# Order of the last overlapped turn and of the tail in a fused two-layer gated cross-attention kernel: one output projection, one turning step and half an output product in other places

## The chip, the cores and the metric

The kernel runs on one core of one Trainium2 chip. The metric is the time of one execution in microseconds (us), from device timestamps; lower is better. Besides that time there is one execution taken by the hardware profiler. Its span runs from the first to the last instruction, and its own time is a little longer than its span.

## The reference

The input is x, of shape 8 x 256 x 512 (eight batches), and a context of the same shape. Four residual layers follow each other, each with a layer norm before it and tanh of a gate as its factor:

```python
x = x + tanh(g_xattn[0]) * L0_xattn(layernorm(x), ctx, ctx)   # causal attention, 16 heads of 32
x = x + tanh(g_ffn[0])   * L0_ffn(layernorm(x), ...)          # ternary weights, 512 -> 2 x 2048 -> 512
x = x + tanh(g_xattn[1]) * L1_xattn(layernorm(x), ctx, ...)   # q projection, rms norms, softmax, output projection
x = x + tanh(g_ffn[1])   * L1_ffn(layernorm(x), ...)          # 8-bit activations, ternary weights
```

The last layer is what the tail of the kernel computes: the normed input is scaled by 127 over its largest absolute value and rounded, multiplied with ternary weights into a value and a gate of 2048 columns each, u = value * silu(gate); u is scaled and rounded in the same way (which needs the largest absolute value over a whole row) and multiplied with ternary output weights.

## The kernel before, in words

There are four stages, a to d, one for each layer. Stages c (second attention) and d (last feed-forward) are interleaved: in a turn, attention of batch b, the output projection of batch c = b-1 and the feed-forward of batch d = b-2 run side by side. Turns 3 to 7 are a loop; the eighth turn is written out, with b = 7, c = 6, d = 5, and no further batch to prepare. Behind it comes the tail, in which batches 6 and 7 pass through the feed-forward. A batch has 256 rows, that is two tiles of 128 (t = 0, 1).

Each engine has its own program, in which every instruction stands in the order written by hand and waits on semaphores. TensorE's program names these steps; each has a counterpart with its name, or a related one, on VectorE (DVE) and ScalarE (ACT):

- c_scores(b, g): attention scores of four heads, group g of 4, into banks 0 to 3; VectorE takes row maxima (L1652).
- c_max_turn(b): the negated maxima, turned (L763). VectorE's c_max_parts prepares them and c_max_rows (L1667) copies the turned ones back.
- c_probs(b, g): scores again, transposed (L773) plus maxima (L777), for four heads; ScalarE takes the exponentials in two instructions (L1192).
- c_weigh(b, g): weighted values and sums (L792); VectorE divides (L1683 reciprocal, L1685 product).
- c_project_out(b, t): output projection (L699), 4 matmuls of 128x512 f32, recorded as 8. VectorE adds it to x (c_add_out, L1690).
- d_value_gate(d, j), j = 0 to 7: 4 matmuls for a gate and 4 for a value (L804), 512 columns, four j for each tile. ScalarE makes silu of the gate (d_gate, L1209), VectorE the product u (L1753) and after every second j a maximum over 1024 columns (L1759).
- d_scale_u (L1765 to L1769): the scale of u from those maxima, six dependent small instructions. ScalarE's d_round_u (L1221) scales and rounds, in two halves of 1024 columns; VectorE's d_integers16 (L1778) writes them as 16-bit.
- d_turn_u(d, t): 16 transposes (L434) of the rounded u, eight to a bank (steps ut t.0 and ut t.1); ScalarE copies each bank out (d_turn_u, L1227, recorded under the helper's line L1012).
- d_out_product(d, t, first, end): 16 matmuls (L834) of the output product, or one half of them; the second eight need the second copy. VectorE's d_store (L1797) adds to x, and SyncE stores it.

PSUM has 8 banks. Banks 0 to 3 belong to the scores and probabilities until the eighth turn ends. The strings in places.turn give the order in which the steps take banks 4 to 7 (one string for each bank; w0 is c_weigh 0's, mt c_max_turn's, po c_project_out's, ut d_turn_u's). A step waits until the step named before it in the same string has been read out. The list ends does the same for the tail, going round all eight banks. The step before in the string is therefore a wait, wherever it is read late:

```python
def d_turn_u(d, t, n):                                        # ScalarE, L1223
    act.wait_ge(s.d_ut, 4 * d + 2 * t + n + 1)
    copy(UT[d, t][:, n * 1024:(n + 1) * 1024], ...).then_inc(s.d_utr, 1)
```

In the eighth turn ScalarE's program is: exponentials 0, a rounding, exponentials 1, a rounding, exponentials 2, a rounding, exponentials 3, then the copies of d_turn_u.

Of the kernel before, what the change touches and what calls it, by code (L numbers as in the profile page):

```python
# [17 lines left out]
KH = HID // P  # L18
NB = 8
# [6 lines left out]
NG = NH // 4  # L26
# [126 lines left out]
def build(nc, x, ctx, ctxT, gates, w0, w1, wkv, wqo, vec, wnorm, cols, cst, masks, selq, selc, out):  # L153
    with ExitStack() as stack:
# [112 lines left out]
        for turn in range(3, NB):  # L267
            places.turn(turn, ("g0 v1 g3 pq0 v6 v7 ut0.0 y0 xt0", "v0 po1 v3 g4 v5 g7 tq1 w1 w2 w3", "po0 g2 kt0 v4 pq1 w0 qt1 ut1.1 y1",
                               "g1 v2 kt1 g5 g6 mt tq0 ut0.1 qt0 ut1.0 xt1"))
        places.turn(NB, ("g0 v1 g3 v5 v7 w1 w3", "v0 po1 v3 g6 g7 ut0.0 y0", "po0 g2 g4 g5 mt w0 ut0.1", "g1 v2 v4 v6 w2"))  # L270
        places.last.update({n: (s.c_ex, 8 * NB) for n in range(4)})
        a, b, c = NB - 3, NB - 2, NB - 1
        ends = ([("po0", c), ("ut1.0", a), ("ut1.1", a), ("po1", c), ("qt0", b), ("qt1", b), ("y1", a)]
                + [(f"{what}{j}", b) for j in range(6) for what in "gv"] + [("qt0", c), ("qt1", c)]
                + [(f"{what}{j}", b) for j in (6, 7) for what in "gv"] + [("g0", c), ("v0", c), ("g1", c), ("v1", c)]
                + [("ut0.0", b), ("ut0.1", b), ("g2", c), ("v2", c), ("y0", b), ("g3", c), ("v3", c), ("ut1.0", b), ("ut1.1", b), ("g4", c), ("v4", c)]
                + [("g5", c), ("v5", c), ("ut0.0", c), ("ut0.1", c), ("g6", c), ("v6", c), ("g7", c), ("v7", c)]
                + [("y1", b), ("y0", c), ("ut1.0", c), ("ut1.1", c), ("y1", c)])
        for k, (name, batch) in enumerate(ends):
            places.put((0, 1, 2, 3, 4, 6, 7, 5)[k % 8], name, batch)  # L280

# [149 lines left out]
        def tensor_program(pe):  # L431
# [278 lines left out]
            def c_project_out(b, t):  # L710
                pe.wait_ge(s.c_pvr, 4 * b + 4)
                c_product(f"po{t}", b, bufC["OT"], t, "o").then_inc(s.c_po, 1)
# [31 lines left out]
            def c_scores(b, g):  # L744
                QT, KT = (bufW[n][:, b % 2 * KD + g, :] for n in ("QT", "KT"))
                pe.wait_ge(s.c_qtr, 4 * b + 4)
                pe.wait_ge(s.c_ktr, 2 * b + 2)
                pe.wait_ge(s.c_scr, 4 * b + g)
                if b == 0:
                    pe.wait_ge(s.b_h, 8 * NB)  # L750
                pe.wait_ge(s.c_ex, 8 * b)
                for t in range(TB):
                    for j in range(4):
                        mm = pe.matmul(banks[j][:, t * S:(t + 1) * S], part(QT, j)[:, t * P:(t + 1) * P], part(KT, j),  # L754
                                       start=(t == 0), stop=(t == 1), skip_group_check=True)
                mm.then_inc(s.c_sc, 1)

            def c_max_turn(b):
                to, sem, value = bank_c("mt", b)
                pe.wait_ge(sem, value)  # L760
                pe.wait_ge(s.c_mhl, b + 1)
                for t in range(TB):
                    mm = pe.transpose(as16(to, BF16)[:, t * P:(t + 1) * P], bufC["MHL"][:, t, :], keep["identb"])  # L763
                mm.then_inc(s.c_mt, 1)
# [31 lines left out]
            def d_value_gate(d, j):  # L796
                t, n = j // 4, j % 4
                pe.wait_ge(s.d_qtr, 2 * d + t + 1)
                for name, col, done in ((f"g{j}", HID + n * D, s.d_g), (f"v{j}", n * D, s.d_gu)):
                    to, sem, value = bank_c(name, d)  # L800
                    pe.wait_ge(sem, value)
                    for k in range(KD):
                        at = k * 2 * HID + col
                        mm = pe.matmul(to, QQ[d][:, t, k * P:(k + 1) * P], W1[:, at:at + D],  # L804
                                       start=(k == 0), stop=(k == KD - 1))
                    mm.then_inc(done, 1)
# [155 lines left out]
            c_project_out(c, 0)  # L962
            d_value_gate(d, 1)
            c_scores(b, 1)
            c_project_out(c, 1)
            d_value_gate(d, 2)
            c_scores(b, 2)
            d_value_gate(d, 3)
            d_value_gate(d, 4)
            c_scores(b, 3)  # L970
            d_value_gate(d, 5)
            d_value_gate(d, 6)
            c_max_turn(b)
            d_value_gate(d, 7)
            for g in range(NG):
                c_probs(b, g)
                if g:
                    c_weigh(b, g - 1)
            d_turn_u(d, 0)
            c_weigh(b, 3)  # L980
            d_out_product(d, 0)
            c_project_out(b, 0)
            d_turn_u(d, 1)
            c_project_out(b, 1)
# [13 lines left out]
            d_turn_u(c, 1)  # L998
            d_value_gate(b, 4)
            d_value_gate(b, 5)  # L1000
            d_turn_u(b, 0)
            d_value_gate(b, 6)
            d_value_gate(b, 7)
            d_out_product(c, 1)
            d_out_product(b, 0, 0, KH // 2)
            d_turn_u(b, 1)
            d_out_product(b, 0, KH // 2)
            d_out_product(b, 1)

        def scalar_program(act):  # L1010
# [309 lines left out]
            d_gate(d, 1)  # L1320
            d_residual(d, 0)
            d_residual(d, 1)
            for j in range(2, 8):
                d_gate(d, j)
            warm(ACT.Exp)
            c_probs(b, 0)
            d_round_u(d, 0, 0)
            c_probs(b, 1)
            d_round_u(d, 0, 1)
            c_probs(b, 2)  # L1330
            d_round_u(d, 1, 0)
            c_probs(b, 3)
            warm(ACT.Silu)
            both(d_turn_u, d, 0)
            d_round_u(d, 1, 1)
            both(d_turn_u, d, 1)
            d_residual(c, 0)
            d_residual(c, 1)
# [25 lines left out]
        def vector_program(v):  # L1364
# [381 lines left out]
                    v.tensor_scalar(bufC["q16"][:, t, :], bufC["h"][:, t, :], MAGIC, 127.0, ALU.subtract, ALU.min).then_inc(s.d_q, 1)  # L1746

            def d_value_gate(d, j):
                t, n = j // 4, j % 4
                v.wait_ge(s.d_sv, d + 1)  # L1750
                v.wait_ge(s.d_gu, 8 * d + j + 1)
                v.wait_ge(s.d_sg, 8 * d + j + 1)
                v.scalar_tensor_tensor(out=bufW["u"][:, t, n * D:(n + 1) * D], in0=bank_c(f"v{j}", d)[0], scalar=keep["sv"][:, d % 2, t:t + 1],  # L1753
                                       in1=bufC["SG"][:, n % 2, :], op0=ALU.mult, op1=ALU.mult).then_inc(s.d_u, 1)
                apart = (d, t) == (NB - 1, 1) and n > 1
                if n % 2 or apart:
                    first, m = (n, n - 1) if apart else (n - 1, n // 2)
                    v.wait_ge(s.d_u, 8 * d + j + 1)
                    v.tensor_reduce(keep["um"][:, t, m:m + 1], bufW["u"][:, t, first * D:(n + 1) * D], AX_X, ALU.max, apply_absolute_value=True).then_inc(*own.up())  # L1759
# [205 lines left out]
            c_add_out(c, 0)  # L1965
            d_value_gate(d, 1)
            c_scores(b, 1)
            c_add_out(c, 1)
            v.wait_ge(s.c_xo, 2 * c + 2)
            d_spread(c)  # L1970
            d_value_gate(d, 2)
            c_scores(b, 2)
            d_value_gate(d, 3)
            d_value_gate(d, 4)
            c_scores(b, 3)
            c_max_parts(b)
            d_scale_u(d, 0)
            d_value_gate(d, 5)
            c_max_rows(b)
            d_value_gate(d, 6)  # L1980
            d_value_gate(d, 7)
            d_scale_u(d, 1)
            d_weighted(c)
            c_weigh(b, 0)
            d_integers16(d, 0)
            c_weigh(b, 1)
            d_peak(c)
            c_weigh(b, 2)
            c_weigh(b, 3)
            d_inputs(c)  # L1990
            d_integers16(d, 1)
            d_store(d, 0)
            c_add_out(b, 0)
            c_add_out(b, 1)
# [208 lines left out]
```

## Time and profile before

| what | us |
|---|---|
| median of three runs | 1124.33 |
| lowest and highest | 1123.89, 1126.89 |
| the profiled execution's own time | 1122.95 |
| its span | 1121.0 |
| TensorE (PE) busy | 1093.6 |
| VectorE (DVE) busy | 832.5 |
| ScalarE (ACT) busy | 567.4 |

A row of the timeline has start, length (both us), engine, line, operation, output<-inputs and shape, and a count where like instructions are merged; in brackets the idle time of the engine before it and what ended it. Merged matmuls overlap: the start of the next row, not the length, tells when the engine went on. A row of the windows gives busy time of an engine and number of instructions begun, and PEclk, the granted TensorE clock (1.00 is 2.4 GHz, 0.50 is 1.2 GHz).

### The profile page before, as it was taken

How to read it: one execution, taken by the hardware profiler on the slowest of the kernel's cores; microseconds unless marked ns; L12 is line 12 of the kernel's file. 1: busy time of each engine (PE TensorE's matmuls, PEld its weight loads, DVE VectorE, ACT ScalarE, POOL GpSimd, SP SyncE). 2: the span in 40 equal slices, each digit the busy share in tenths (PEclk: the TensorE clock that was granted, in tenths of full speed). 3: DMA queues.
4: the chain of work that ended last, by engine and by line, in shares of the span. 5: the costliest groups of instructions: out<-in, count | busy, mean ns of one | idle time of the engine just before them, and what ended most of it. 6: DMA issues, size and time to landing. Idle time of an engine off the chain costs nothing.

```text
span 1121.0 us, 25577 instructions
## 1 busy us (share of the span) xinstructions
PE 1093.6 (98%) x10386; PEld 661.7 (59%) x10386; DVE 832.5 (74%) x1437; ACT 567.4 (51%) x918; POOL 117.3 (10%) x212
## 2 busy tenths in 40 slices
PE   8899999999999999999999999999999999999998
PEld 3455555556777777777777655555554545454543
DVE  4888888778676657566565667986868787778795
ACT  4767666765433323333333352464554547372654
POOL 1101100110000000000001122120202020201010
PEclk9999999999999999999999999999999999999999
DMA  9655555433212011021010201101010101000001
GB/s 361 205 188 182 187 190 174 147 107 124 67 39 66 20 39 38 20 76 38 20 58 20 85 1 39 39 2 57 1 58 1 58 1 39 1 11 10 11 10 38
DMA packets 29267, 79.24 MB, mean 71 GB/s; under 512 B 3040, under 2 KB 3296, under 8 KB 28896
## 3 DMA queue, kind: packets, MB, share of 16 engines
q1 hardware_dynamic: 29152, 77.61, 21.2%
q8 instruction: 84, 1.38, 0.5%
q14 instruction: 31, 0.25, 0.1%
HBM read 65.02 MB, written 12.58 MB: 69 GB/s over the span
## 4 chain that ended last, share of the span: by engine, by line
PE 91%; DVE 4%; ACT 2%; issue 2%; DMA 1%; SPq 0%; POOL 0%; ACTq 0%; DVEq 0%; POOLq 0%
PE bank L699 10%; PE bank L593 10%; PE bank L594 10%; PE bank L681 10%; PE bank L554 9%; PE bank L804 9%; PE bank L434 5%; PE bank L834 5%; PE bank L792 5%; PE bank L754 3%; PE bank L773 3%; PE bank L486 2%; PE bank L459 2%; PE bank L507 2%; PE bank L519 2%
## 5 line engine op out<-in xcount | busy, mean ns | idle before, releaser
L593 PE MATMUL bank<-ARENA,W 128*128 128x256 f16 x1024 | 227.3, 273 | 0.7 <-issue 0.7
L594 PE MATMUL bank<-ARENA,W 128*128 128x256 f16 x1024 | 227.3, 273 | 0.0
L1012 ACT ACTIVATE ARENA<-bank 128x512 f32<-128x512 f32 (+3 forms) x143 | 93.0, 687 | 71.7 <-PE bank L434 31.8
L681 PE MATMUL bank<-W,ARENA 128*128 128x512 bf16 x512 | 120.8, 379 | 0.0
L804 PE MATMUL bank<-W,ARENA 128*128 128x512 bf16 x512 | 119.3, 383 | 0.4 <-DVE W L1753 0.4
L554 PE MATMUL bank<-ARENA 128*128 128x512 f32 x256 | 117.8, 602 | 0.7 <-DMA ARENA<-in_wkv 0.7
L699 PE MATMUL bank<-ARENA 128*128 128x512 f32 x256 | 116.9, 599 | 0.0
L593 PEld LDWEIGHTS bank<-ARENA,W 128*128 128x128 bf16 x1024 | 100.2, 98 | 19.1 <-issue 1.3
L594 PEld LDWEIGHTS bank<-ARENA,W 128*128 128x128 bf16 x1024 | 100.2, 98 | 18.0
L1012 ACT ACTIVATE ARENA<-ARENA 128x512 f16<-128x512 f32 x64 | 40.3, 630 | 133.2 <-DVE ARENA L1607 129.5
L2031 POOL TENSOR_TENSOR ARENA<-ARENA 128x2 f32<-128x2 f32 (+1 forms) x72 | 49.6, 689 | 507.1 <-DVE ARENA L1387 267.4
L1607 DVE SCALAR_TENSOR_TENSOR ARENA<-bank,ARENA 128x512 f32<-128x512 f32 x64 | 48.0, 750 | 72.5 <-PE bank L594 69.1
L1209 ACT ACTIVATE ARENA<-bank,ARENA 128x512 f32<-128x512 f32 x64 | 43.7, 685 | 109.1 <-PE bank L804 101.3
L804 PEld LDWEIGHTS bank<-W,ARENA 128*128 128x128 bf16 x512 | 49.2, 99 | 67.1 <-issue 15.0
L1130 ACT ACTIVATE ARENA<-bank 128x512 f32<-128x512 f32 x64 | 38.2, 597 | 91.1 <-PE bank L594 91.1
L1652 DVE TENSOR_REDUCE ARENA<-bank 128x4 f32<-128x1024 f32 x64 | 75.2, 1218 | 9.4 <-PE bank L754 9.4
L1613 DVE TENSOR_TENSOR ARENA<-ARENA 128x512 f16<-128x512 f32 x64 | 44.2, 691 | 47.3 <-ACT ARENA L1012 47.3
L554 PEld LDWEIGHTS bank<-ARENA 128*128 128x128 f32 x256 | 46.6, 190 | 54.7 <-issue 51.1
L681 PEld LDWEIGHTS bank<-W,ARENA 128*128 128x128 f16 x512 | 50.0, 99 | 48.7 <-issue 1.9
L1683 DVE RECIPROCAL ARENA<-bank 128x256 f32<-128x256 f32 x32 | 56.2, 1755 | 29.5 <-PE bank L792 29.2
L1397 DVE TENSOR_REDUCE ARENA<-bank 128x4 f32<-128x512 f32 x64 | 58.2, 951 | 26.5 <-PE bank L459 26.5
L699 PEld LDWEIGHTS bank<-ARENA 128*128 128x128 f32 x256 | 46.6, 190 | 52.6 <-issue 51.6
(181 smaller groups left out, 1801.9 us busy)
## 6 DMA issues: line engine op xcount, KB each, us to landing
W<-in_w SPq DMA_DIRECT2D x48, 512.0 KB, 4.3
ARENA<-in_w SPq DMA_DIRECT2D x24, 512.0 KB, 3.6
kv_store<-ARENA SPq DMA_DIRECT2D x32, 256.0 KB, 4.3
W<-kv_store SPq DMA_DIRECT2D x15, 512.0 KB, 4.0
ARENA<-in_ctxT SPq DMA_DIRECT2D x8, 512.0 KB, 3.8
X<-in_x SPq DMA_DIRECT2D x8, 512.0 KB, 6.1
ARENA<-in_ctx SPq DMA_DIRECT2D x8, 512.0 KB, 6.1
out<-X SPq DMA_DIRECT2D x16, 256.0 KB, 2.0
```

The costliest lines, as they stand in the source:

```text
L434: mm = pe.transpose(to[:, k * P:(k + 1) * P], tile, one)
L554: mm = pe.matmul(bank, bufA["KT"][:, b % 2 * KD + k, t * P:(t + 1) * P], W[:, k, :], start=(k == 0), stop=(k == KD - 1))
L593: pe.matmul(bank[:, i * S:(i + 1) * S], W0[:, at:at + P], xt_half(b, 0)[:, k, :], start=(k == 0), stop=False)
L594: mm = pe.matmul(bank[:, i * S:(i + 1) * S], W0[:, at:at + P], xt_half(b, 1)[:, k, :], start=False, stop=(k == KD - 1))
L681: mm = pe.matmul(banks[6 + t], hx(q, what)[:, i * S + t * P:i * S + (t + 1) * P], W0[:, UP_AT + m * D:UP_AT + (m + 1) * D], start=(m == 0 ...
L699: mm = pe.matmul(to, src[:, k, t * P:(t + 1) * P], WQ[w][:, k, :], start=(k == 0), stop=(w == "o" and k == KD - 1))
L792: mm = pe.matmul(part(to, j)[:, what * S:(what + 1) * S], lhs, bufC["PT"][:, h % 8, kb * S:(kb + 1) * S], start=(kb == 0), stop=True, skip ...
L804: mm = pe.matmul(to, QQ[d][:, t, k * P:(k + 1) * P], W1[:, at:at + D], start=(k == 0), stop=(k == KD - 1))
L1012: return act.activation(to, src, ACT.Copy)
L1397: got = v.tensor_reduce(NM[:, t, :, g % 2], bank[:, 0:4, t * P:t * P + (t + 1) * P], AX_X, ALU.max, negate=True)
L1652: got = v.tensor_reduce(NM[:, t, :, g], bank[:, 0:4, t * S:(t + 1) * S], AX_X, ALU.max, negate=True)
L1683: v.reciprocal(bufC["rec"], to[:, S:2 * S]).then_inc(*own.up())
```

## The change

In the eighth turn, c_project_out(6, 1) moves from behind scores 1 to behind c_max_turn. d_turn_u(5, 0) moves from behind weighing 2 to between probabilities 0 and probabilities 1, and the first half of the output product of (5, 0) to before weighing 3. On ScalarE the two roundings of (5, 0) move from between the exponentials to before gates 6 and 7, the two copies of the turned values to between exponentials 1 and 2, and the roundings of (5, 1) behind the exponentials. VectorE's order follows; d_value_gate is split there into the product and the maximum. The bank strings of the turn change with it: po1 goes behind g7 in bank 5, and in bank 6 ut0.1 now stands before w0. In the tail, the first half of the output product of (6, 1) moves before d_turn_u(7, 0), and the output product of (7, 0) stands whole before d_turn_u(7, 1), of which its second half was the successor. In the list ends, ("y1", b) moves forward, which shifts the banks of all that come after it: ut1.0 of batch 7 now follows y1 of batch 6 in bank 2.

```diff
--- before.py
+++ after.py
@@ -267,15 +267,15 @@
         for turn in range(3, NB):
             places.turn(turn, ("g0 v1 g3 pq0 v6 v7 ut0.0 y0 xt0", "v0 po1 v3 g4 v5 g7 tq1 w1 w2 w3", "po0 g2 kt0 v4 pq1 w0 qt1 ut1.1 y1",
                                "g1 v2 kt1 g5 g6 mt tq0 ut0.1 qt0 ut1.0 xt1"))
-        places.turn(NB, ("g0 v1 g3 v5 v7 w1 w3", "v0 po1 v3 g6 g7 ut0.0 y0", "po0 g2 g4 g5 mt w0 ut0.1", "g1 v2 v4 v6 w2"))
+        places.turn(NB, ("g0 v1 g3 v5 v7 w1 w3", "v0 v3 g6 g7 po1 ut0.0 y0", "po0 g2 g4 g5 mt ut0.1 w0", "g1 v2 v4 v6 w2"))
         places.last.update({n: (s.c_ex, 8 * NB) for n in range(4)})
         a, b, c = NB - 3, NB - 2, NB - 1
         ends = ([("po0", c), ("ut1.0", a), ("ut1.1", a), ("po1", c), ("qt0", b), ("qt1", b), ("y1", a)]
                 + [(f"{what}{j}", b) for j in range(6) for what in "gv"] + [("qt0", c), ("qt1", c)]
                 + [(f"{what}{j}", b) for j in (6, 7) for what in "gv"] + [("g0", c), ("v0", c), ("g1", c), ("v1", c)]
                 + [("ut0.0", b), ("ut0.1", b), ("g2", c), ("v2", c), ("y0", b), ("g3", c), ("v3", c), ("ut1.0", b), ("ut1.1", b), ("g4", c), ("v4", c)]
-                + [("g5", c), ("v5", c), ("ut0.0", c), ("ut0.1", c), ("g6", c), ("v6", c), ("g7", c), ("v7", c)]
-                + [("y1", b), ("y0", c), ("ut1.0", c), ("ut1.1", c), ("y1", c)])
+                + [("g5", c), ("v5", c), ("y1", b), ("ut0.0", c), ("ut0.1", c), ("g6", c), ("v6", c), ("g7", c), ("v7", c)]
+                + [("y0", c), ("ut1.0", c), ("ut1.1", c), ("y1", c)])
         for k, (name, batch) in enumerate(ends):
             places.put((0, 1, 2, 3, 4, 6, 7, 5)[k % 8], name, batch)
 
@@ -962,23 +962,24 @@
             c_project_out(c, 0)
             d_value_gate(d, 1)
             c_scores(b, 1)
+            d_value_gate(d, 2)
+            d_value_gate(d, 3)
+            c_scores(b, 2)
+            d_value_gate(d, 4)
+            d_value_gate(d, 5)
+            c_scores(b, 3)
+            d_value_gate(d, 6)
+            d_value_gate(d, 7)
+            c_max_turn(b)
             c_project_out(c, 1)
-            d_value_gate(d, 2)
-            c_scores(b, 2)
-            d_value_gate(d, 3)
-            d_value_gate(d, 4)
-            c_scores(b, 3)
-            d_value_gate(d, 5)
-            d_value_gate(d, 6)
-            c_max_turn(b)
-            d_value_gate(d, 7)
-            for g in range(NG):
+            c_probs(b, 0)
+            d_turn_u(d, 0)
+            for g in range(1, NG):
                 c_probs(b, g)
-                if g:
-                    c_weigh(b, g - 1)
-            d_turn_u(d, 0)
+                c_weigh(b, g - 1)
+            d_out_product(d, 0, 0, KH // 2)
             c_weigh(b, 3)
-            d_out_product(d, 0)
+            d_out_product(d, 0, KH // 2)
             c_project_out(b, 0)
             d_turn_u(d, 1)
             c_project_out(b, 1)
@@ -998,13 +999,13 @@
             d_turn_u(c, 1)
             d_value_gate(b, 4)
             d_value_gate(b, 5)
+            d_out_product(c, 1, 0, KH // 2)
             d_turn_u(b, 0)
             d_value_gate(b, 6)
             d_value_gate(b, 7)
-            d_out_product(c, 1)
-            d_out_product(b, 0, 0, KH // 2)
+            d_out_product(c, 1, KH // 2)
+            d_out_product(b, 0)
             d_turn_u(b, 1)
-            d_out_product(b, 0, KH // 2)
             d_out_product(b, 1)
 
         def scalar_program(act):
@@ -1320,19 +1321,19 @@
             d_gate(d, 1)
             d_residual(d, 0)
             d_residual(d, 1)
-            for j in range(2, 8):
+            for j in range(2, 6):
                 d_gate(d, j)
+            both(d_round_u, d, 0)
+            d_gate(d, 6)
+            d_gate(d, 7)
             warm(ACT.Exp)
             c_probs(b, 0)
-            d_round_u(d, 0, 0)
             c_probs(b, 1)
-            d_round_u(d, 0, 1)
+            both(d_turn_u, d, 0)
             c_probs(b, 2)
-            d_round_u(d, 1, 0)
             c_probs(b, 3)
             warm(ACT.Silu)
-            both(d_turn_u, d, 0)
-            d_round_u(d, 1, 1)
+            both(d_round_u, d, 1)
             both(d_turn_u, d, 1)
             d_residual(c, 0)
             d_residual(c, 1)
@@ -1746,12 +1747,19 @@
                     v.tensor_scalar(bufC["q16"][:, t, :], bufC["h"][:, t, :], MAGIC, 127.0, ALU.subtract, ALU.min).then_inc(s.d_q, 1)
 
             def d_value_gate(d, j):
+                d_gated(d, j)
+                d_largest(d, j)
+
+            def d_gated(d, j):
                 t, n = j // 4, j % 4
                 v.wait_ge(s.d_sv, d + 1)
                 v.wait_ge(s.d_gu, 8 * d + j + 1)
                 v.wait_ge(s.d_sg, 8 * d + j + 1)
                 v.scalar_tensor_tensor(out=bufW["u"][:, t, n * D:(n + 1) * D], in0=bank_c(f"v{j}", d)[0], scalar=keep["sv"][:, d % 2, t:t + 1],
                                        in1=bufC["SG"][:, n % 2, :], op0=ALU.mult, op1=ALU.mult).then_inc(s.d_u, 1)
+
+            def d_largest(d, j):
+                t, n = j // 4, j % 4
                 apart = (d, t) == (NB - 1, 1) and n > 1
                 if n % 2 or apart:
                     first, m = (n, n - 1) if apart else (n - 1, n // 2)
@@ -1965,30 +1973,31 @@
             c_add_out(c, 0)
             d_value_gate(d, 1)
             c_scores(b, 1)
+            d_value_gate(d, 2)
+            d_value_gate(d, 3)
+            c_scores(b, 2)
+            d_scale_u(d, 0)
+            d_value_gate(d, 4)
+            d_gated(d, 5)
+            c_scores(b, 3)
+            c_max_parts(b)
+            d_largest(d, 5)
+            d_gated(d, 6)
+            c_max_rows(b)
+            d_integers16(d, 0)
+            d_value_gate(d, 7)
             c_add_out(c, 1)
+            d_scale_u(d, 1)
             v.wait_ge(s.c_xo, 2 * c + 2)
             d_spread(c)
-            d_value_gate(d, 2)
-            c_scores(b, 2)
-            d_value_gate(d, 3)
-            d_value_gate(d, 4)
-            c_scores(b, 3)
-            c_max_parts(b)
-            d_scale_u(d, 0)
-            d_value_gate(d, 5)
-            c_max_rows(b)
-            d_value_gate(d, 6)
-            d_value_gate(d, 7)
-            d_scale_u(d, 1)
+            c_weigh(b, 0)
             d_weighted(c)
-            c_weigh(b, 0)
-            d_integers16(d, 0)
             c_weigh(b, 1)
             d_peak(c)
             c_weigh(b, 2)
             c_weigh(b, 3)
+            d_integers16(d, 1)
             d_inputs(c)
-            d_integers16(d, 1)
             d_store(d, 0)
             c_add_out(b, 0)
             c_add_out(b, 1)
```

## Rows read from the trace of the kernel before

**Rows 1.** The page, section 1: busy time and its share of the span.
```profile
PE 1093.6 (98%) x10386; PEld 661.7 (59%) x10386; DVE 832.5 (74%) x1437; ACT 567.4 (51%) x918; POOL 117.3 (10%) x212
```

**Rows 2.** Waits of TensorE, 900 to 1121 us: us in total, times, longest.
```profile
PE bank L434 <- DVE ARENA L1778: 2.0, 2, 1.6
PE bank L773 <- ACT ARENA L1192: 1.8, 3, 1.3
PE bank L792 <- DVE ARENA L1685: 1.3, 1, 1.3
PE bank L773 <- DVE ARENA L1667: 0.4, 1, 0.4
PE bank L804 <- DVE W L1753: 0.4, 1, 0.4
```

**Rows 3.** Timeline of TensorE in the eighth turn.
```profile
1036.60 1.15 PE L773 MATMUL bank<-W 32*128 32x256 f32 x16 [0.41 <-DVE ARENA L1667]
...
1039.24 1.74 PE L773 MATMUL bank<-W 32*128 32x256 f32 x14 [1.28 <-ACT ARENA L1192]
...
1041.35 1.07 PE L792 MATMUL bank<-ARENA,W 128*32 128x256 f32 x16
...
1049.96 1.07 PE L434 MATMUL bank<-ARENA 128*128 128x128 bf16 x16
1050.96 1.07 PE L792 MATMUL bank<-ARENA,W 128*32 128x256 f32 x16
1051.85 1.05 PE L792 MATMUL bank<-ARENA 128*32 128x256 f32 x16
1052.83 3.63 PE L834 MATMUL bank<-W,ARENA 128*128 128x512 bf16 x16
1056.29 3.60 PE L699 MATMUL bank<-ARENA 128*128 128x512 f32 x8
```

**Rows 4.** Timeline of ScalarE in the eighth turn: exponentials 1, a rounding, two copies.
```profile
1041.45 1.94 ACT L1192 ACTIVATE ARENA<-bank 128x1024 f32<-128x1024 f32 x2 [0.40 <-PE bank L777]
1043.27 1.15 ACT L1221 ACTIVATE W<-W,ARENA 128x1024 f32<-128x1024 f32 x1
...
1051.56 1.92 ACT L1012 ACTIVATE ARENA<-bank 128x1024 bf16<-128x1024 bf16 x2
```

**Rows 5.** Timeline of VectorE: division after weighing 3; one scan of scores.
```profile
1030.50 2.35 DVE L1652 TENSOR_REDUCE ARENA<-bank 128x4 f32<-128x1024 f32 x2
...
1052.96 1.76 DVE L1683 RECIPROCAL ARENA<-bank 128x256 f32<-128x256 f32 x1 [0.65 <-PE bank L792]
1054.75 0.42 DVE L1685 TENSOR_TENSOR ARENA<-bank,ARENA 128x256 f32<-128x256 f32 x1
```

**Rows 6.** Timeline of TensorE in the tail.
```profile
1094.41 3.62 PE L804 MATMUL bank<-W,ARENA 128*128 128x512 bf16 x16
1099.64 0.61 PE L434 MATMUL bank<-ARENA 128*128 128x128 bf16 x8 [1.61 <-DVE ARENA L1778]
1100.68 0.61 PE L434 MATMUL bank<-ARENA 128*128 128x128 bf16 x8 [0.43 <-DVE ARENA L1778]
1101.12 5.30 PE L804 MATMUL bank<-W,ARENA 128*128 128x512 bf16 x16
1106.26 5.34 PE L834 MATMUL bank<-W,ARENA 128*128 128x512 bf16 x24
1111.44 1.06 PE L434 MATMUL bank<-ARENA 128*128 128x128 bf16 x16
1112.34 5.34 PE L834 MATMUL bank<-W,ARENA 128*128 128x512 bf16 x24
```

**Rows 7.** Timeline of VectorE and ScalarE in the tail.
```profile
1106.52 0.75 DVE L1753 SCALAR_TENSOR_TENSOR W<-bank,ARENA 128x512 f32<-128x512 f32 x1 [0.50 <-PE bank L804]
...
1111.30 0.74 DVE L1797 SCALAR_TENSOR_TENSOR X<-bank,ARENA,X 128x512 f32<-128x512 f32 x1
...
1112.09 1.02 ACT L1012 ACTIVATE ARENA<-bank 128x1024 bf16<-128x1024 bf16 x1 [1.64 <-PE bank L434]
```

**Rows 8.** Windows of TensorE: us, busy, granted clock (PEclk), DMA share, GB/s.
```profile
1003.00:1006.00 3.00, 1.66 (x33) 1.00 0.03 5
1038.00:1041.00 3.00, 1.63 (x20) 1.00 0.00 0
1101.50:1104.50 3.00, 3.00 (x9) 0.50 0.00 0
1104.85:1106.26 1.41, 1.41 (x8) 1.00 0.00 0
```

**Rows 9.** The only earlier fall of the clock: a timeline row, then two windows.
```profile
35.71 0.30 PE L444 MATMUL bank<-ARENA 32*128 32x64 bf16 x16 [2.35 <-ACT ARENA L1012]
...
34.00:36.00 2.00, 0.29 (x20) 1.00 0.61 94
36.00:38.00 2.00, 1.90 (x30) 0.61 0.92 348
```

## What the change should do to the time

> **What bounds the kernel now.** I read the page's busy times first. TensorE is busy for 1093.6 of 1121.0 us, 98% [rows 1], so a reordering can gain only what TensorE stands still or runs slowly around the edit. The waits of TensorE from 900 us on give the stock [rows 2]. In the eighth turn these are 0.39 us before value 7, 0.41 us for the turned maxima and 1.28 us for the exponentials; in the tail 1.61 and 0.43 us for the rounded values. The 1.3 us behind a division lies at 1004 us, ahead of the edit, and stays. The timeline then shows the places [rows 3, 6]. The windows show something no wait row does: from about 1101.5 to 1104.8 us the granted clock is 0.50, the 1.2 GHz level [rows 8]. Sixteen matmuls that start at 1101.12 go on to 1106.26, that is 5.14 us [rows 6]; at full clock 24 take 1106.26 to 1111.44 = 5.18 us, 0.216 each, so 16 take 3.45. The slow stretch costs 1.69 us. What came before it was 1.61 and 0.43 us of idleness within 2.65 us.
>
> **The eighth turn up to probabilities 0: about nothing.** The output projection (3.43 to 3.5 us, the row of its sister at 1056.29 is followed by transposes 3.43 us later) moves behind the maxima, where it covers VectorE's copy of them (the 0.41 us wait). In exchange everything between comes 3.45 us earlier and meets VectorE and ScalarE. VectorE scans each of the four scores for 2.35 us [rows 5], and ScalarE now does two roundings of 1.04 us each (a rounding of 1.15 us, pipelined) before gate 6. Played through in order from the second scan, which starts at 1019.96 in both: scan 2.27, two products and a maximum 2.6, scan 2.27, scale 1.2 brings the scale to 1028.3, two roundings to 1030.4, silu of gate 6 to 1031.1. TensorE would have got to gate 7 at 1030.1 and needs the bank of gate 6: 1.0 us idle. From 1031.2: value and gate 7 1.73, maxima 0.25, projection 3.45 gives 1036.65 for probabilities 0, against 1036.60 now [rows 3]. The two short waits are only replaced by one of 1.0 us. Bounds: minus 0.8 us (no new wait), plus 0.7 us; I take 0.05.
>
> **Turned values between the probabilities: a new wait of 3.9 us.** This decides. Bank 6 is now read by ut0.1 before w0 takes it. Weighing 0 thus waits for ScalarE's second copy, and in ScalarE's program both copies stand behind exponentials 1. Exponentials 1 need probabilities 1, whose matmuls need exponentials 0, so they start when they do now, at 1041.45, and the next instruction of ScalarE starts at 1043.27 [rows 4]. The two copies take 1.92 us [rows 4]: 1045.19, and 0.06 until TensorE goes on, 1045.25. TensorE's own work up to weighing 0 ends at 1041.35, where weighing 0 starts now [rows 3]; the transposes (1.0 us) fit into the stretch in which it waits for the exponentials anyway, from 1037.9 to the end of probabilities 1, even if their first bank, which the moved projection's addition frees, comes some 0.5 us late. Weighing 0 is late by 3.90 us. Queued behind it on TensorE are probabilities 2 and all that follows; VectorE has nothing to divide either.
>
> A rule of the Trainium skill speaks to this place: "TensorE: Matmul & The Clock Gate", in its part on engine queue depths, says that ScalarE and VectorE are strict FIFO and that on TensorE only weight loads are pulled ahead of matmuls. By it the copy cannot pass the exponentials and weighing 0 cannot be passed by probabilities 2, so the wait stands in full; could either pass, the turn would cost about 3.6 us less. No row of this case shows an engine passing one over.
>
> **The rest of the turn.** The transposes no longer stand between weighings 2 and 3: minus 1.00 us (1049.96 to 1050.96) [rows 3]. Half an output product, 8 x 0.216 = 1.73 us, goes in ahead of weighing 3, so only the other half lies between weighing 3 and the next output projection. That projection needs the last division: it starts 0.13 us after weighing 3 and ends 2.34 us after it (1052.83 to 1055.17) [rows 3, 5], plus 0.14 us to TensorE, 2.48. A whole product of 3.46 us covers that, half does not: 2.48 - 1.73 = 0.75 us idle. The later roundings of (5, 1) are ready by then (they were last at 1054.5, and would be at about 1057, with integers by 1060 and their transposes wanted at 1063): nothing. The statistics of batch 6 and GpSimd's line behind them come later by the projection's move, but the next gates, 10 us on, are the first to need them; SyncE's stores move with VectorE's and end before the last one: nothing. Sum of the turn: 0.05 + 3.90 - 1.00 + 0.75 = 3.70 us later.
>
> **The tail at full clock.** Half the product of (6, 1), 1.73 us, fills the 1.61 us of idleness. The second group of transposes still waits for VectorE's second half, at 1100.68 in the old times, so gate 6 starts when it did, at 1101.12, with eight matmuls fewer behind it. Values 7 end; then 8 + 16 matmuls of output products stand before the last transposes, 24 as now [rows 6]. But their bank is now the one that y1 of batch 6 leaves, and VectorE stores that behind the last integers. From product 7 to the end of this store it takes 1106.52 to 1112.04 = 5.52 us [rows 7]; TensorE comes 5.18 us after 1106.26. The start is (1112.04 + 0.14) - 1111.44 = 0.74 us late. Then the last output product follows the transposes at once. Their first copy now starts 0.65 us after the transposes and takes 1.02 (1112.09, first transposes at 1111.44) [rows 6, 7]; plus 0.06 it is 1.73 us, against 0.90 us of transposes: 0.83 us idle, where the other half product was the cover. Sum: -1.73 + 0.74 + 0.83 = -0.16 us.
>
> **The clock.** The idle 2.04 us of the tail shrinks to 0.3, so its slow stretch should go: -1.69 us. The new 3.9 us hole should bring one. The only earlier fall of the clock came right behind a wait of 2.35 us [rows 9]; the waits of 1.34 and 1.28 us at 1003 and 1038 us were followed by none [rows 8]. Its price is between 0.9 us (part of the slow stretch lies in the hole itself, where nothing runs) and 1.69 (all of it on work), 2.4 if it is prolonged, 0 if none comes. I take 1.3, nearest to the two slow stretches seen.
>
> The page "TensorE: Matmul & The Clock Gate", section "What's actually happening", says that the slow rate is the default and that activity releases it; it agrees with a fall after a hole and would leave the sum as it is.
>
> **The sum.** 3.70 - 0.16 - 1.69 + 1.3 = +3.15 us. Against the profiled execution's own time this is 1122.95 + 3.15 = 1126.1. Its three unprofiled runs have a median 1.38 us higher; the forecast for the median is 1124.33 + 3.15 = 1127.5, 0.28% slower.
>
> **Rivals.** (A) The forecast's mechanism, with the slow stretch for 0.9 to 2.4 us: 1127.1 to 1128.6, chance 0.60. Rows 4 and the bank order speak for it, both nearly beyond doubt; its size lies at the edge of what can be measured.
> (B) The hole without a fall of the clock: +1.85, 1126.2, chance 0.15. Against it stand rows 9.
> (C) The hole, its slow stretch, and another in the last 5 us, where 0.74 and 0.83 us of idleness now stand close together with only transposes between them: 1.7 us more, 1129.2. For it: the tail's fall came after idleness of 2.04 us around transposes. Against: 1.57 is nearer to the 1.3 us waits that did nothing. Chance 0.13.
> (D) Not slower: the wait of weighing 0 does not come last. It decides from where the two copies would be done by 1041.35, so they would have to start by 1039.4, while exponentials 1 start at 1041.45. Then the turn is +0.05 - 1.00 + 0.75 plus some 0.5 us by which exponentials 2 come late behind the copies, about +0.3, and the tail -1.85: 1122.8, chance 0.08. Only if in addition the replaced waits of the turn vanish (-0.8) and the 0.75 and 1.57 us of new ones are hidden would it reach 1119.7; chance 0.04.
>
> A measurement of this kernel can tell about 0.3%, 3.4 us, from no change. Slower by more is half of A's 0.60 at most (0.28), C, and a part of what the unprofiled runs scatter: 0.45. Faster by more is the last case and a little for what the trace does not show: 0.06. The rest, 0.49, is within. The range takes in B, C and, half way, D: 1122.8 to 1130.0.
>
> **What would show it.** In the new trace: weighing 0 (L792) with a wait of about 3.9 us for ScalarE's L1012 near 1041 to 1045 us; a granted clock of 0.5 behind it; a wait of 0.7 to 0.8 us of L699 for L1685; no clock below 1.00 at the tail's gates 6 and 7, and no wait of 1.6 us there; before the last 16 matmuls waits of about 0.7 us for L1797 and 0.8 us for L1012. The forecast is wrong if the first of these is missing or under 2 us, and off by its clock terms if the slow stretches lie elsewhere.

## The result and the profile after

The changed kernel takes 1127.89 us (median of 11 runs), the kernel before 1123.58 (median of 11); the ratio is 1.0039, 95% interval 1.003 to 1.0047. It is slower, by 4.3 us by the medians and 4.4 by the ratio, where 3.15 had been forecast. The time lies within the range of the forecast (1122.8 to 1130.0) and 0.4 us above its centre of 1127.5. The changed kernel's profiled execution took 1128.76 us with a span of 1126.7. One later execution of the kernel before took 1403.4 us at a mean clock of 0.752, in a second, slower state, and is left out of all ratios and counts.

First the waits of TensorE from 900 us on (us in total, times, longest):

```profile
PE bank L792 <- ACT ARENA L1013: 3.9, 1, 3.9
PE bank L792 <- DVE ARENA L1686: 1.3, 1, 1.3
PE bank L804 <- ACT ARENA L1210: 0.8, 1, 0.8
PE bank L773 <- ACT ARENA L1193: 0.8, 3, 0.3
PE bank L834 <- ACT ARENA L1013: 0.8, 1, 0.8
PE bank L699 <- DVE ARENA L1686: 0.5, 1, 0.5
PE bank L434 <- DVE X L1805: 0.5, 1, 0.5
```

Against [rows 2], the waits of 1.61 us for rounded values, 1.28 for exponentials and 0.41 for the maxima are gone. In their place stands one of 3.86 us of weighing 0 (L792) for a copy (L1013, the line L1012 of before), and four single ones of 0.5 to 0.8 us. The 1.3 us one lies ahead of the edit in both. The timeline of TensorE in the eighth turn, then of ScalarE:

```profile
1011.09 1.15 PE L754 MATMUL bank<-W 32*128 32x256 f32 x16
...
1032.50 1.89 PE L804 MATMUL bank<-W,ARENA 128*128 128x512 bf16 x8 [0.80 <-ACT ARENA L1210]
...
1038.08 1.15 PE L773 MATMUL bank<-W 32*128 32x256 f32 x16
...
1046.75 1.94 PE L792 MATMUL bank<-ARENA,W 128*32 128x256 f32 x16 [3.86 <-ACT ARENA L1013]
1048.46 1.93 PE L792 MATMUL bank<-ARENA 128*32 128x256 f32 x16
1050.33 1.86 PE L773 MATMUL bank<-W 32*128 32x256 f32 x16
...
1052.33 1.07 PE L792 MATMUL bank<-ARENA,W 128*32 128x256 f32 x16
...
1063.76 3.70 PE L699 MATMUL bank<-ARENA 128*128 128x512 f32 x8 [0.51 <-DVE ARENA L1686]
```

```profile
1042.93 1.94 ACT L1193 ACTIVATE ARENA<-bank 128x1024 f32<-128x1024 f32 x2 [1.44 <-PE bank L777]
1044.75 1.95 ACT L1013 ACTIVATE ARENA<-bank 128x1024 bf16<-128x1024 bf16 x2
```

Exponentials 1 start, the two copies follow, they end at 1046.70, weighing 0 starts at 1046.75. Its two halves last 1.94 and 1.93 us each, where they lasted 1.07 [rows 3]: these matmuls ran at half the clock. In the kernel before, probabilities 2 followed weighing 0, and weighing 1 followed them, at these times:

```profile
1043.21 1.15 PE L773 MATMUL bank<-W 32*128 32x256 f32 x14
...
1044.72 1.07 PE L792 MATMUL bank<-ARENA,W 128*32 128x256 f32 x16
```

The windows of TensorE (us, busy, granted clock, DMA share, GB/s) show from where to where:

```profile
1044.50:1045.00 0.50, 0.00 (x0) 0.99 0.00 0
1045.00:1045.50 0.50, 0.00 (x0) 0.50 0.00 0
...
1051.50:1052.00 0.50, 0.50 (x12) 0.68 0.00 0
1052.00:1052.50 0.50, 0.50 (x16) 1.00 0.00 0
...
1107.00:1117.50 10.50, 10.06 (x58) 1.00 0.01 2
```

The clock is low from 1045.0 to about 1051.8, and the last line shows the tail at full clock, where [rows 8] had 0.50. The timeline of the tail:

```profile
1105.44 1.89 PE L834 MATMUL bank<-W,ARENA 128*128 128x512 bf16 x8
1107.22 0.61 PE L434 MATMUL bank<-ARENA 128*128 128x128 bf16 x8
1108.26 0.61 PE L434 MATMUL bank<-ARENA 128*128 128x128 bf16 x8 [0.43 <-DVE ARENA L1786]
1108.70 3.62 PE L804 MATMUL bank<-W,ARENA 128*128 128x512 bf16 x16
1112.15 5.34 PE L834 MATMUL bank<-W,ARENA 128*128 128x512 bf16 x24
1117.99 1.07 PE L434 MATMUL bank<-ARENA 128*128 128x128 bf16 x16 [0.49 <-DVE X L1805]
1119.82 3.61 PE L834 MATMUL bank<-W,ARENA 128*128 128x512 bf16 x16 [0.76 <-ACT ARENA L1013]
```

The first scores of the eighth turn in the kernel before, from the timeline:

```profile
1009.81 1.15 PE L754 MATMUL bank<-W 32*128 32x256 f32 x16
```

VectorE's last addition, which the last store waits for, from the chain that ended last, before and after (start, us, what):

```profile
1117.72 0.75 DVE X L1797
```

```profile
1123.47 0.75 DVE X L1805
```

To take the difference apart, count from these first scores (1009.81 before, 1011.09 after; the 1.28 us between them arose ahead of the edit, and in the twelve profiles taken they start between 1009.8 and 1011.7 us). Probabilities 0 start 0.20 us later than before, weighing 0 4.12 us, the output projection behind the turn 6.19, gate 6 of the tail (1101.12 and 1108.70) 6.30, the first of the 24 matmuls (1106.26 and 1112.15) 4.61, the last addition (1117.72 and 1123.47) 4.47 us.

### The profile page after: what moved, and what is told of

Same layout as the page of the kernel before. It is cut to its first block, busy times and chain, and to the rows that moved or that the text cites. A ratio compares the mean times of both kernels' runs of the same rounds, so it can differ in the third digit from the quotient of the medians.

```text
span 1126.7 us, 25578 instructions
## 1 busy us (share of the span) xinstructions
PE 1094.4 (97%) x10386; PEld 662.0 (59%) x10386; DVE 832.1 (74%) x1437; ACT 567.2 (50%) x918; POOL 116.7 (10%) x212
## 4 chain that ended last, share of the span: by engine, by line
PE 90%; DVE 4%; ACT 3%; issue 2%; DMA 1%; SPq 0%; POOL 0%; ACTq 0%; DVEq 0%; POOLq 0%
PE bank L699 10%; PE bank L593 10%; PE bank L594 10%; PE bank L681 10%; PE bank L554 9%; PE bank L804 9%; PE bank L434 5%; PE bank L792 5%; PE bank L834 4%; PE bank L773 3%; PE bank L754 3%; PE bank L519 2%; PE bank L459 2%; PE bank L486 2%; PE bank L507 2%
## 5 line engine op out<-in xcount | busy, mean ns | idle before, releaser
L1013 ACT ACTIVATE ARENA<-bank 128x512 f32<-128x512 f32 (+3 forms) x143 | 93.0, 687 | 72.6 <-PE bank L434 33.2
L1013 ACT ACTIVATE ARENA<-ARENA 128x512 f16<-128x512 f32 x64 | 40.3, 630 | 133.2 <-DVE ARENA L1608 129.5
```

The lines of the kernel that those rows point to most:

```text
L1013: return act.activation(to, src, ACT.Copy)
```

## The experiments

### The bank of weighing 0

The theory is that the 3.86 us wait is the loss and the slow clock its consequence. It can be removed without touching any order of instructions.

```diff
-"po0 g2 g4 g5 mt ut0.1 w0", "g1 v2 v4 v6 w2"
+"po0 g2 g4 g5 mt w0", "g1 v2 v4 v6 ut0.1 w2"
```

> The changed kernel with one thing other: in the eighth turn ut0.1 takes bank 7 (behind v6, before w2) and w0 follows mt in bank 6 again, so weighing 0 does not wait for ScalarE's copy. Theory (the wait of weighing 0 for the second copy is the loss, and the slow clock is its consequence): the 3.86 us wait goes, the granted clock stays at 1.00 in the turn, exponentials 2 come about 0.4 us late behind the copies; against the changed kernel about -5.7 us, against the kernel before 0.2 - 1.0 + 0.5 + 0.4 in the turn and -1.8 in the tail, -1.7 us (ratio 0.9985). Rival (the moved projection and the early roundings are the loss, the wait only shows it): some other wait of 3 to 4 us of TensorE takes its place between probabilities 1 and 2, and the time stays within 1 us of the changed kernel's, ratio 1.003 to 1.004.

Measured: 1122.3 us, ratio 0.9984 (0.9973 to 0.9994). The wait is gone and no other of its size came; the largest in the turn is the 0.8 us before gate 7, and the granted clock is 1.00 from 1030 to 1060 us. The theory holds and the rival falls: by the medians one bank's order costs 5.6 us, by the ratios 6.2, more than the whole change costs (4.4).

### The copies first

The same hole, closed from the other side: banks as in the changed kernel, ScalarE's order other.

```diff
 c_probs(b, 0)
+both(d_turn_u, d, 0)
 c_probs(b, 1)
-both(d_turn_u, d, 0)
 c_probs(b, 2)
```

> The changed kernel with ScalarE's two copies of the turned values before exponentials 1 instead of behind them; banks as in the changed kernel. Theory (it is the place of the copies in ScalarE's order that opens the hole): weighing 0 can start some 0.5 us after probabilities 1, exponentials 1 come 1.8 us later but are hidden behind weighing 0 (1.86 us); no slow clock; against the changed kernel -5.3 us, against the kernel before -1.3 us, ratio 0.9988. Rival (delayed exponentials cost as much as the hole did): a wait of 1.5 to 2 us moves to probabilities 2, and the ratio is 1.000 or more.

Measured: 1121.64 us, ratio 0.9986 (0.9977 to 0.9995). The wait of weighing 0, in the timeline of TensorE:

```profile
1042.09 1.07 PE L792 MATMUL bank<-ARENA,W 128*32 128x256 f32 x16 [0.48 <-ACT ARENA L1013]
```

It is 0.48 us, and the first half of weighing 0 lasts 1.07 us, as at full clock. ScalarE's exponentials 1 now run while TensorE weighs; probabilities 2 wait for nothing. All 10 executions have a mean clock (the granted clock averaged over the whole execution) of 0.998, even one that took 1124.2 us. One reading aid: each of the twelve profiles taken also has a slow stretch near its start, beginning between 35 and 42 us. In eleven it lasts 3.4 us, as in [rows 9], which takes 0.0015 off the mean. So 0.998 means that one stretch, 0.997 one more of this length, 0.995 two more, and the mean does not tell where they are. ScalarE does the same work in both kernels; only the place of 1.95 us in its order differs, and it moves the end by 6 us (6.2 by the medians, 6.0 by the ratios). This is what the Trainium skill's statement of strict FIFO on ScalarE ("TensorE: Matmul & The Clock Gate", section "Architectural detail: the array is 16× 32×32, not 1× 128×128", on engine queue depths) would have it do, and the two runs agree with it.

### A shorter hole

```diff
-c_probs(b, 1)
-both(d_turn_u, d, 0)
+c_probs(b, 1, lambda: both(d_turn_u, d, 0))    # copies between its two exponentials
```

> The changed kernel with ScalarE's two copies between the two instructions of exponentials 1: the hole before weighing 0 shrinks from 3.86 to 2.95 us. Theory (a hole of 2 to 4 us lowers the clock in every execution, for a stretch that does not depend much on its length): -0.9 us against the changed kernel, mean clock 0.995 as there, ratio to the kernel before about 1.003. Rival (the slow stretch is as long as it is because the hole is: it shrinks to half with it): -0.9 - 1.7 us, mean clock 0.997, ratio 1.0015.

Measured: 1126.72 us, ratio 1.0028 (1.0019 to 1.0037). The hole is 2.94 us; mean clocks are 0.995 in six of ten executions, 0.997 in two, 0.996 and 0.993 in one each, against 0.995 in eight of eleven for the changed kernel. By medians and ratios the gain of about 1.2 us is the hole's 0.9 and little more, which is nearer to the theory. In its profile, though, the slow stretch of the turn was short:

```profile
1045.50:1046.00 0.50, 0.00 (x0) 0.70 0.00 0
...
1049.00:1049.50 0.50, 0.50 (x12) 0.89 0.00 0
```

That is 3.4 us against 6.8 in the changed kernel's profile. From the first scores of the turn to the end of the span it took 113.6 us, against 115.6: 2.0 us less, where the rival had 2.6 and the theory 0.9. That this execution still had the lowest mean clock of the ten, 0.993, comes from its start, where the clock was at 0.50 for 10.2 us:

```profile
33.00:36.00 3.00, 0.65 (x33) 0.89 0.40 72
36.00:39.00 3.00, 3.00 (x52) 0.50 0.97 351
...
45.00:48.00 3.00, 2.30 (x36) 0.90 0.62 228
```

So neither theory nor rival is decided here, and a mean clock cannot be put down to the turn without a profile.

### The changed kernel once more

> The changed kernel once more, for a second profile. Theory: the wait of weighing 0 is 3.86 us again to 0.05 us, a slow stretch follows it again, but where it begins and how long it lasts differs by up to 3 us. Rival: the stretch begins 2 us into the hole and lasts 6.7 us again, and so belongs to the hole's length.

```profile
1043.00:1043.50 0.50, 0.00 (x0) 0.91 0.00 0
...
1050.00:1050.50 0.50, 0.50 (x12) 0.76 0.00 0
```

These are windows of this second profile of the changed kernel. The wait is again 3.85 us (from 1041.7 to 1045.5), 1127.34 us in all. The stretch lasts from about 1043.4 to 1050.25, 6.8 us again, and begins 1.7 us into the hole, against 2.1 before. On length and place that is the rival's forecast rather than the theory's. The profile of the turn alone, below, has the same length, but its stretch begins 0.7 us into the hole, so the place is not fixed. With three profiles at 3.9 us and one at 2.9 the hole's length may well set the stretch's; the shorter hole's mean clocks, 0.995 in most executions, speak against that, as far as they tell of the turn. What a stretch costs is the part of it that lies on work behind the hole: by the times of these profiles 5.1 and 4.7 us in the two of the changed kernel, 3.7 in the turn alone, 2.7 behind the shorter hole, of which rather less than half is lost (2.2 of the 5.1 us). The clock falls in each such hole; how much work the slow stretch covers is not fixed by what was measured here.

### The tail alone

```diff
 # the kernel before, with the list `ends` and TensorE's tail of the changed one
+d_out_product(c, 1, 0, KH // 2)
 d_turn_u(b, 0)
...
-d_out_product(c, 1)
-d_out_product(b, 0, 0, KH // 2)
-d_turn_u(b, 1)
-d_out_product(b, 0, KH // 2)
+d_out_product(c, 1, KH // 2)
+d_out_product(b, 0)
+d_turn_u(b, 1)
```

> The kernel before with only the tail's edit (half the output product of (6, 1) moved ahead, the product of (7, 0) whole before the last transposes, the bank list). Theory: the 1.61 us wait is filled and the slow clock at gates 6 and 7 goes (-1.69 us), while waits of 0.5 us for the store and 0.8 us for the copy come before the last transposes and the last product: -1.8 us, ratio 0.9984. Rival (the slow stretch near the end has another cause than the idleness just before it): clock 0.50 somewhere between 1095 and 1110 us again, and a time within 0.3 us of the kernel before.

Measured: 1123.46 us, ratio 0.9996 (0.9983 to 1.0009): no difference that can be told. In the profile the tail itself does what was expected; its clock is 1.00 from 1095 to 1110 us and the waits are 0.50 and 0.97 us. In this execution the gain was lost elsewhere, in the part that was not edited. Windows of this kernel, then its timeline in the eighth turn:

```profile
1039.50:1040.00 0.50, 0.50 (x4) 0.60 0.00 0
1040.00:1040.50 0.50, 0.50 (x8) 0.50 0.00 0
...
1046.00:1046.50 0.50, 0.50 (x8) 0.58 0.00 0
```

```profile
1036.79 1.15 PE L773 MATMUL bank<-W 32*128 32x256 f32 x16 [0.41 <-DVE ARENA L1667]
...
1039.43 2.48 PE L773 MATMUL bank<-W 32*128 32x256 f32 x14 [1.28 <-ACT ARENA L1192]
```

The same waits of 0.41 and 1.28 us stand here as in [rows 3], and behind them the clock is low for 6.8 us. From probabilities 0 to the output projection it takes 22.48 us (1036.79 to 1059.27) against 19.69 [rows 3]: 2.8 us. In the first profile of the kernel before the same waits had been followed by full clock [rows 8].

### The kernel before, twice more

> The kernel before once more, for another profile. Theory (the short waits of the eighth turn, 0.4 and 1.3 us, sometimes lower the clock, as they did in the run of the tail alone, and in the first profile did not): the same waits to within 0.1 us, and the slow stretches in other places or of other length than in the first profile. Rival (the slow stretches belong to fixed places): 1.7 us of loss at gates 6 and 7 of the tail and none in the turn, as in the first profile.

> The kernel before a third time, for the same question: theory, slow stretches differ again in place or length with the same waits; rival, they are where they were in the first profile.

Windows of TensorE, of the second and then of the third profile:

```profile
1038.00:1048.00 10.00, 8.60 (x120) 0.83 0.01 2
1095.00:1110.00 15.00, 12.68 (x74) 0.89 0.05 17
```

```profile
1038.00:1048.00 10.00, 8.60 (x144) 1.00 0.01 2
1095.00:1110.00 15.00, 12.91 (x71) 1.00 0.05 17
```

The waits agree within 0.1 us, the clock does not. The second (1125.46 us) is slow for 3.4 us in the turn and for 3.4 us in the tail; the third (1121.59) in neither, with the same 1.61 and 0.43 us waits; the first profile, with 1122.95 us, in the tail alone. So a slow stretch is not the certain consequence of the 2.0 us of idleness in the tail, as the prediction had it, nor are 1.3 us free of it. The mean clock of each execution shows the mixture. Of the 62 executions of the kernel before that were run beside the experiments, 8 have 0.998 (median 1121.5 us), 31 have 0.997 (1123.0), 15 have 0.995 (1124.6), 7 have 0.994 (1125.9) and one has 0.992 (1126.9).

### The turn alone, as changed and mended

```diff
 # the changed kernel, with the list `ends` and TensorE's tail of the kernel before
```

> The changed kernel with the tail as before. Theory: the turn costs +6.3 us (4.0 of waits moved, 2.3 of slow clock) and the tail keeps its 1.61 us wait and, if idleness sets it, its own slow stretch of 1.7 us: against the kernel before +6.3 us, ratio 1.0056. Rival (only one slow stretch comes, wherever the first hole is): the tail stays at full clock and the ratio is near 1.004.

Measured: 1128.47 us, ratio 1.0037 (1.0025 to 1.0049), mean clocks 0.994 and 0.995. The profile has both stretches: the clock is 0.5 in the turn for 6.8 us at a wait of 3.85 us, and in the tail for 3.4 us from 1107.6 on, with the 1.61 us wait ahead of it. So the rival's mechanism falls; yet the ratio came out at the rival's value. The likely reason is that the theory's 6.3 us came from the first profile pair, whose execution of before has no slow stretch in the turn, while the typical one already pays for part of it. The ratio is no higher than the changed kernel's (1.0037 and 1.0039): behind this turn the tail's edit brings nothing that can be told.

With the copies first, and the tail as before:

> The eighth turn as changed, with the copies first, and the tail as before. It splits the gain of the kernel with the copies first (ratio 0.9986). Theory (at full clock the mended turn is worth nothing, +0.2 - 1.0 + 0.5 + 0.5 = +0.2 us, and takes the chance of a slow stretch out of the turn, while the tail keeps its own): the fastest executions are at 1121.7, like those of the kernel before, most have one slow stretch, median near 1123.0, ratio 0.9993. Rival (the turn is all of the gain, the tail none): ratio 0.9986 again and every execution within 0.5 us of 1121.7.

Measured: 1122.52 us, ratio 0.999 (0.9979 to 1.0000). Six of ten executions have clock 0.998, median 1122.1, four 0.997, median 1123.4. By the ratios the mended turn brings 1.1 us, and the new tail 0.45 us more (0.9 by the medians, from runs on two chips); with these intervals either could be a microsecond more or less. I had expected most executions to have a slow stretch in the tail; 6 of 10 had none. At equal mean clock (0.998) the mended turn is 0.6 us slower than the kernel before (1122.1 against 1121.5): it removes no work from the path. Four profiles say the same: from the turn's first scores to the end of the span it takes 110.0 us, and 109.8 and 109.7 with the new tail (copies first, other bank), against 109.5 in the third profile of the kernel before. What the mended turn gains is that the clock no longer falls in the turn, where no wait is longer than 0.8 us: none of these profiles has a slow stretch there, and all ten executions with the copies first have 0.998. The kernel before has 0.998 in 8 of 62 executions, with the new tail alone in 3 of 10, with the mended turn alone in 6 of 10. These counts suggest that its turn loses more often than its tail; ten executions each do not prove it.

### A better version

The tail's two new waits, 0.49 and 0.76 us, were put down to a bank's order and to missing cover. Both can be mended.

```diff
 # the kernel with the copies first
-[("g5", c), ("v5", c), ("y1", b), ("ut0.0", c), ("ut0.1", c), ("g6", c), ...
+[("g5", c), ("v5", c), ("ut0.0", c), ("ut0.1", c), ("y1", b), ("g6", c), ...
...
-d_out_product(b, 0)
+d_out_product(b, 0, 0, 12)
 d_turn_u(b, 1)
+d_out_product(b, 0, 12)
```

> The kernel with the copies first, and the tail mended: y1 of batch 6 is listed two places later, so the last transposes no longer follow it in its bank, and the output product of (7, 0) is cut at 12 of 16 matmuls, 4 of them behind the last transposes as cover for the copy. Theory (the new waits of 0.5 and 0.8 to 1.0 us in the tail are the bank order and the missing cover): the last transposes wait about 0.35 us for the rounded values, the last product for nothing; 24 matmuls and waits of 1.25 us become 24 matmuls and 0.35 us, -0.9 us against the kernel with the copies first, ratio to the kernel before 0.9978. Rival (VectorE's chain behind value 7 sets the end whatever TensorE does): a wait of 1.3 us for the rounded values, and no gain.

Timeline of TensorE in its tail:

```profile
1105.16 4.48 PE L834 MATMUL bank<-W,ARENA 128*128 128x512 bf16 x20
1109.83 1.21 PE L434 MATMUL bank<-ARENA 128*128 128x128 bf16 x16 [0.18 <-DVE ARENA L1787]
1111.09 4.26 PE L834 MATMUL bank<-W,ARENA 128*128 128x512 bf16 x19
```

Measured: 1120.71 us (12 executions, all at mean clock 0.998), ratio 0.9976 (0.9967 to 0.9985). The last transposes wait 0.18 us and the last product for nothing. The bank's order and the cover were changed together, so what each is worth was not measured. This is the fastest version measured: 2.7 us below the kernel before by the ratio, and 7 us below the changed one. It is faster at equal mean clock (0.998) too, by 0.8 us (1120.7 against 1121.5).

## Why the prediction was right, and where it was off

**The wait of weighing 0.** Forecast 3.90 us, measured 3.86, and by the starts 3.92 (4.12 - 0.20). The bank string, ScalarE's order and two rows of durations were enough. The two mended kernels, one with another bank and one with another order on ScalarE, show that this order is the cause.

**The turn up to probabilities 0.** Forecast +0.05 us with a new wait of 1.0 us before gate 7; measured +0.20 with a wait of 0.80.

**The rest of the turn at full clock.** Forecast -0.25 (less 1.00, plus 0.75). Weighing 0 took 3.58 us instead of 1.86, probabilities 2 2.00 instead of 1.51, together 2.21 us of slow clock; the projection came 6.19 - 4.12 = 2.07 us later, so -0.14 without it. Right in the sum; the projection's wait was 0.51 us where 0.75 had been forecast, and the output product, cut in two, took 0.26 us longer, which was not in the sum.

**The tail at full clock.** Forecast -0.16. From gate 6 on it gained 6.30 - 4.47 = 1.83 us, of which the 16 slow matmuls of before are 1.69: -0.14. The last transposes came 5.84 us after the first of the 24 matmuls instead of 5.18 (0.66 late, forecast 0.74), the last product 1.83 us after them instead of 0.90 (0.93, forecast 0.83).

**The clock is the term that was mis-sized.** I took 1.3 us for the slow stretch behind the new hole, with 2.4 as the upper bound; it took 2.2, since it lasted 6.8 us and not the 3.4 that the tail had shown, part of it in the hole. Those 0.9 us are most of the distance from 3.15 to the 4.47 us of the two profiles; the rest is mainly three small amounts of 0.1 to 0.15 us. The step behind it was weaker than it looked: I read from one profile that waits of 1.3 us leave the clock alone and that 2 us of idleness bring it down. Both readings were chance. For the tail as a whole -1.85 us was forecast, of which -1.69 for the clock were taken as certain; it is worth 0.45 us by the ratios and 0.9 by the medians with the turn mended, and on the kernel before it brings nothing measurable. The sum came out near because the errors pull against each other: a dearer slow stretch in the turn and less gain in the tail than forecast, but a typical kernel before that already loses in the turn. That the time came within 0.4 us of 1127.5 is in part luck: the change itself was missed by 1.2 us (3.15 forecast, 4.3 and 4.4 measured), and the median of the kernel before, 1124.33 us in three runs, came out at 1123.58 in eleven. The changed kernel's profiled execution took 1128.76 us where 1126.1 had been forecast; 1.28 us of that arose ahead of the edit.

**The rivals.** (B), the hole without a fall of the clock, did not occur in either profile. (C), another slow stretch behind the tail's new waits, was not seen in any profile; one execution in eleven, with a mean clock of 0.992, may have had it, or a longer slow stretch at its start. (D) fell: the wait came last. The kernels that come near D's condition, one with the copies done 0.48 us after weighing 0 is due and one in which it does not wait for them, give 1121.6 and 1122.3 us, near D's 1122.8.

**What stays open.** Why the same waits lower the clock in one execution and not in the next, and what sets the length of a slow stretch (those in the turn and the tail were all near 3.4 or 6.8 us), was not settled. Behind the same 1.28 us wait the clock fell 0.2 us after its end in one profile (tail alone), 1.5 us after it in another (the kernel before, second), and not at all in two. The moved projection was not run by itself.

## What to carry to other kernels

When a step is moved between two others, read the buffer order as a wait and follow it into the reader's own queue: two copies of 1.95 us together cost a wait of 3.9 us here because they stood behind exponentials that themselves came late, and exchanging the order of one bank or of one engine gave it all back. On an engine that is 98% busy, short waits can cost more than their length, since here some of them were followed by a lower clock; judge their price from the times and mean clocks of many executions, and use profiles, more than one, to see where the clock was low. When the work between a value and its use is moved ahead, keep as much behind as its longest latency needs: 20 of 24 matmuls ahead and 4 behind, with a bank freed earlier, beat 24 ahead.

## What the runs showed of the hardware

The kernel before, unchanged, ran at 1121.6, 1122.95 and 1125.5 us in three profiles, with the same waits and with none, one and two slow stretches of TensorE in its last 90 us. A wait of 1.28 us, with one of 0.41 us shortly before it, was followed in two profiles of four by a stretch at 0.50 of the clock, once for 6.8 us at a cost of 2.8 us. Waits of 1.61 and 0.43 us close together in the tail were followed by one of 3.4 us in three profiles of five. Stretches that began in holes of 3.86, 3.85, 3.85 and 2.94 us lasted 6.8, 6.8, 6.8 and 3.4 us, and began 2.1, 1.7, 0.7 and 2.2 us into them.
